# Moving routing work of an expert mixture from VectorE to ScalarE and GpSimd, and delaying work in the last attention unit

## The reference

```python
z = jnp.einsum('nd,sdr->nsr', xf, P)            # xf: layernorm of h; S=8 spaces, R=16
scores = jnp.einsum('nsr,smr->nsm', z, C)       # M=64 experts a space
topv, topi = jax.lax.top_k(scores, K)           # K=4
w = jax.nn.softmax(topv, axis=-1)
...
h = jax.nn.gelu(jnp.einsum('nsr,nskrh->nskh', z, W1g) + b1g)
yl = jnp.einsum('nskh,nskhr->nskr', h, W2g) + b2g
comb = jnp.einsum('nskr,nsk->nsr', yl, w)
out = jax.nn.gelu(comb @ G1 + g1b) @ G2 + g2b
```

## Time and profile before

| | us |
|---|---|
| median of 3 runs | 2743.81 |
| lowest, highest | 2742.77, 2745.2 |
| the profiled execution | 2734.5 |
| its span | 2732.8 |

### The profile page before, as it was taken

One profiled execution on the slowest core, in us unless ns is written; L12 is line 12 of the kernel. 1 busy time (PEld: TensorE's weight loads), 2 busy tenths in 40 slices (PEclk: granted clock), 3 DMA queues, 4 the chain that ended last, 5 costly groups with the idle time before them and its releaser, 6 DMA issues. The chain is left out here.

```text
span 2732.8 us, 42139 instructions
## 1 busy us (share of the span) xinstructions
PE 2409.2 (88%) x16000; PEld 1217.6 (45%) x16000; DVE 1920.0 (70%) x3888; ACT 1211.1 (44%) x1624; POOL 1142.5 (42%) x774
## 2 busy tenths in 40 slices
PE   3475899999999999999999999767988898898888
PEld 1132565555555555655555555433233232232332
DVE  5873675656565565656565656658889989989998
ACT  3332233333333333333333333345666667677766
POOL 5000275757575766667575757451112111211010
PEclk9787999999999999999999999987899999999999
DMA  1002000000001000000000010220000000000000
GB/s 48 12 16 65 1 8 9 1 9 1 9 1 32 1 9 1 9 2 8 9 1 3 1 19 1 42 62 20 20 15 19 8 19 20 14 18 9 18 7 7
DMA packets 43081, 39.42 MB, mean 14 GB/s; under 512 B 26880, under 2 KB 35328, under 8 KB 41984
## 3 DMA queue, kind: packets, MB, share of 16 engines
q1 hardware_dynamic: 40608, 31.18, 5.1%
q0 software_dynamic: 1536, 3.15, 0.4%
q10 hardware_dynamic: 736, 2.41, 0.2%
HBM read 26.23 MB, written 10.49 MB: 13 GB/s over the span
## 5 line engine op out<-in xcount | busy, mean ns | idle before, releaser
L661 POOL TENSOR_TENSOR acc<-acc,pT 128x1024 f32<-128x1024 f32 (+3 forms) x412 | 835.6, 2028 | 245.5 <-ACT pT L1059 208.4
L1059 ACT ACTIVATE pT<-banks 128x1024 f32<-128x1024 f32 x480 | 406.6, 896 | 835.3 <-PE banks L734 765.6
L1759 DVE TENSOR_TENSOR hw<-hid,banks 128x512 f32<-128x512 f32 x1024 | 665.0, 680 | 74.9 <-PE banks L1454 62.9
L879 DVE TENSOR_REDUCE part<-banks 128x2 f32<-128x1024 f32 (+3 forms) x432 | 438.1, 1044 | 311.6 <-PE banks L710 309.9
L1597 ACT ACTIVATE hid<-banks 128x1024 f32<-128x1024 f32 x512 | 498.5, 1022 | 259.3 <-PE banks L1444 218.7
L1454 PE MATMUL banks<-wT,select 64*128 64x512 f16 x1024 | 358.5, 404 | 74.4 <-DVE hw L1759 49.4
L750 PE MATMUL banks<-pT,v 128*64 128x512 f32 (+3 forms) x1920 | 407.2, 545 | 2.2 <-POOL pT L645 2.2
L1444 PE MATMUL banks<-zst,w1c 50*128 50x512 f32 x1024 | 324.8, 558 | 6.0 <-ACT hid L1597 5.9
L1454 PEld LDWEIGHTS banks<-wT,select 64*128 64x128 f16 x1024 | 95.1, 95 | 456.4 <-DVE hw L1759 368.9
L1462 PE MATMUL banks<-hw,w 128*32 128x512 f32 x2048 | 289.3, 638 | 0.8 <-DVE hw L1759 0.8
L750 PEld LDWEIGHTS banks<-pT,v 128*64 128x64 f32 x1920 | 117.2, 137 | 205.4 <-issue 184.2
(11 more groups left out here) (220 smaller groups left out, 3064.9 us busy)
## 6 DMA issues: line engine op xcount, KB each, us to landing
zst<-z_scratch SPq DMA_DIRECT2D x48, 128.0 KB, 4.1
z_scratch<-zp SPq DMA_DIRECT2D x8, 512.0 KB, 2.8
out_h<-o SPq DMA_DIRECT2D x8, 384.0 KB, 2.6
xT_scratch<-xs_hi SPq DMA_DIRECT2D x4, 512.0 KB, 2.7
xt_hi<-xT_scratch SPq DMA_DIRECT2D x2, 1024.0 KB, 5.6
w<-in_L_ffn_W ACTq DMA_DIRECT2D x1, 2048.0 KB, 8.2
xt_hi<-in_L_ffn_W SPq DMA_DIRECT2D x12, 128.0 KB, 4.4
v<-in_L_ffn_W SPq DMA_DIRECT2D x12, 128.0 KB, 4.7
```

Source lines behind the costliest of these rows:

```text
L661: pool.tensor_tensor(acc[:, G % 2, :, off:CH], acc[:, G % 2, :, off:CH], pT[:, slot, :, 0:w], ALU.add).then_inc(summed, 1)
L879: last = dve.tensor_reduce(to[:, :, c:c + 1], both[:, :, 0:whole], AX.X, ALU.max)
L1059: act.activation(pT[:, J % PSLOTS, :, 0:CH - off], both[:, :, 0:CH - off], ACT.Exp, scale=E ** -0.5)\
L1759: dve.tensor_tensor(hw[:, n % 2, q, :], hid[:, n % 2, q, :], ring_bank(("w", g, n, q)), ALU.mult).then_inc(mixed, 1)
```

## The change

Last attention unit: the output items of chunks 0 to 2 stand six macros behind, not four; prepare(t) stands at the end of VectorE's macro, behind invert and normalise, and most of its pieces in later macros. Experts: row sums and sums of squares go from VectorE (and the square from GpSimd) to ScalarE's accumulating activations, with the small arithmetic of the normalisation and z's split on GpSimd; keep_marked and high_weights go from VectorE to GpSimd as compare, product, product, cast, difference; scores take one bank at a time, in steps 5, 7, 9, 11; z's items stand in steps 14, 15, 17; ScalarE empties the output banks, and g2's bias becomes a 65th row of g2 against a row of ones in gh.

```diff
-        X2_AT, Z_AT = (6, 7), 8
-        NORMALISE_AT = {1: 0, 2: 1, 3: 2, 5: 3}
-        ONES_AT, SPLIT_Z_AT = 4, 9
-        POWER_BEHIND = 8
-        PART_AT = {5: None, 6: 0, 9: 1, 12: 2, 15: 3}
+        X2_AT, Z_AT = (9, 10), 11
+        NORMALISE_AT = {0: 0, 1: 1, 2: 2, 6: 3}
+        ONES_AT, SPLIT_Z_AT = 7, 13
+        POWER_BEHIND = 10
+        PART_AT = {8: None, 9: 0, 12: 1, 14: 2, 16: 3}
+
+        OUT_BEHIND = [4] * LAST + [6]
...
-                unit, t = divmod(it * MACROS + LASTKEY[Q] // 2 + 4, MACROS)
+                unit, t = divmod(it * MACROS + LASTKEY[Q] // 2 + OUT_BEHIND[it], MACROS)
...
                     if it == LAST:
                         sum_odd(2 * t + 1)
-                        prepare(t)
                     if behind(it, t, 2):
                         invert(*behind(it, t, 2), 0)
                     if behind(it, t, 3):
                         invert(*behind(it, t, 3), 1)
                         normalise(*behind(it, t, 3))
+                    if it == LAST:
+                        prepare(t)
...
-        Z_AT = {13: (0,), 14: (1,), 15: (2,)}
-        PREP_AT = {5: (3, 4), 7: (5, 6), 23: (7,), 24: (8,), 26: (9,), 27: (10,)}
+        Z_AT = {14: (0,), 15: (1,), 17: (2,)}
+        PREP_AT = {5: (3,), 7: (4,), 9: (5,), 11: (6,), 23: (7,), 24: (8,), 26: (9,), 27: (10,)}
...
-        KEEP_AT = {(20, 1): 0, (20, 3): 1, (21, 1): 2, (22, 1): 3}
-        HIGH_AT = {(22, 0): 0, (24, 0): 1}
         DEN_AT, RECIPROCALS_AT = (16, 0), (20, 0)
-        SUMS_AT, VARIANCE_AT, REFINE_AT, SPLIT_AT = (6, 0), (8, 0), (10, 0), (18, 0)
-        TAKE_OUT_AT = {(3, 1): 0, (4, 1): 1}
+
+        SUM_AT = {4: 0, 5: 1, 6: 2, 7: 3}
+        SQUARE_AT = {8: 0, 9: 1, 10: 2, 11: 3}
...
             def centre(g):
...
+                pool.wait_ge(summed, g)
+                link(pool.tensor_scalar(neg_mean, total, -1.0 / D, None, ALU.mult))
+                pool.sem_inc(mean_ready, 1)
+                link(pool.tensor_tensor(tok(c[:, :]), tok(h_all[:, g * GW:(g + 1) * GW]), wide(neg_mean), ALU.add))
...
             def scale(g):
-                pool.wait_ge(rstd_ready, g)
+                pool.wait_ge(squared, g)
+                link(pool.tensor_scalar(var, var, 1.0 / D, LNEPS, ALU.mult, ALU.add))
+                link(pool.tensor_tensor(rstd, var, power[:, :], ALU.pow))
+                link(pool.tensor_tensor(newton, rstd, rstd, ALU.mult))
+                link(pool.tensor_tensor(newton, newton, var, ALU.mult))
+                link(pool.tensor_scalar(newton, newton, -0.5, 1.5, ALU.mult, ALU.add))
+                link(pool.tensor_tensor(rstd, rstd, newton, ALU.mult))
                 pool.tensor_tensor(tok(x2[:, :]), tok(c[:, :]), wide(rstd), ALU.mult).then_inc(xn_ready, 1)
...
+            def make_weights(g, part):
...
+                pool.wait_ge(rows_marked, 2 * g + part + 1)
+                pool.tensor_scalar(scr[:, half, 0:M], scr[:, half, 0:M], TAKEN, None, ALU.is_equal)\
+                    .then_inc(kept_step, 1)
+                pool.wait_ge(kept_step, done + 1)
+                pool.wait_ge(exp_done, g + 1)
+                pool.tensor_tensor(ew[:, half, :], ew[:, half, :], scr[:, half, 0:M], ALU.mult).then_inc(kept_step, 1)
+                pool.wait_ge(kept_step, done + 2)
+                pool.wait_ge(rden_ready, g + 1)
                 pool.tensor_tensor(ew[:, half, :], ew[:, half, :],
                                    rden[:, 1, half].unsqueeze(2).to_broadcast([P, GT * S // 2, M]), ALU.mult)\
...
+                pool.tensor_copy(wsp[:, half, :, 0, :], by_half).then_inc(kept_step, 1)
+                pool.wait_ge(kept_step, done + 4)
                 pool.tensor_tensor(wsp[:, half, :, 1, :], by_half, wsp[:, half, :, 0, :], ALU.subtract)\
                     .then_inc(w_ready, 1)
...
                 if g < NG - 2:
-                    normalise(g + 2)
+                    centre(g + 2)
+                    scale(g + 2)
                 if g < NG - 1:
-                    weights(g + 1)
+                    below_best(g + 1)
+                if g < NG - 2:
+                    split_z(g + 2)
+                if g < NG - 1:
+                    for part in range(2):
+                        make_weights(g + 1, part)
...
+            def sum_rows(g, t):
+                if t == 0 and g > 1:
+                    act.wait_ge(xn_ready, g - 1)
+                last = act.activation(sq[:, t * D:(t + 1) * D], h_all[:, (g * GT + t) * D:(g * GT + t + 1) * D],
+                                      ACT.Identity, accum_out=total[:, t:t + 1])
...
+            def square_rows(g, t):
+                if t == 0:
+                    act.wait_ge(mean_ready, g)
+                last = act.activation(sq[:, t * D:(t + 1) * D], h_all[:, (g * GT + t) * D:(g * GT + t + 1) * D],
+                                      ACT.Square, bias=neg_mean[:, t:t + 1], accum_out=var[:, t:t + 1])
...
+            def take_out(g, k):
+                if k == 0:
+                    act.wait_ge(out_stored, g * 16 + 16)
+                bank = bank_in(("out", g, 1 + k))
+                act.activation(tok(o[:, :])[:, 2 * k:2 * k + 2, :],
+                               bank.rearrange("p (t n) -> p t n", t=2)[:, :, 0:D], ACT.Copy).then_inc(out_taken, 1)
...
+            for t in range(GT):
+                sum_rows(1, t)
             for item in FIRST_ITEMS[:4]:
                 take(*item)
+            for t in range(GT):
+                square_rows(1, t)
...
                     if n == EXP_AT and g < NG - 1:
                         exponentials(g + 1)
+                    if n in SUM_AT and g < NG - 2:
+                        sum_rows(g + 2, SUM_AT[n])
+                    if n in SQUARE_AT and g < NG - 2:
+                        square_rows(g + 2, SQUARE_AT[n])
```

More of the change, by code:

```diff
@@ L1197, in stage_experts @@
         comb = sb("comb", [P, GTOK])
-        gh = sb("gh", [GH, GTOK])
-        mean, var, rstd, newton = (small[:, GT * i:GT * i + GT] for i in range(4))
+        gh = sb("gh", [GH + 1, GTOK])
+        total, neg_mean, var, rstd, newton = (small[:, GT * i:GT * i + GT] for i in range(5))
         tok = lambda a: a.rearrange("p (n d) -> p n d", d=D)
@@ L1350, in add_input @@
                 pool.tensor_tensor(o[:, :], o[:, :], h_all[:, g * GW:(g + 1) * GW], ALU.add).then_inc(out_ready, 1)
-            def normalise(g):
-                centre(g)
-                root(g)
-                scale(g)
-            def weights(g):
-                below_best(g)
-                for part in range(2):
-                    divide(g, part)
-                    low_weights(g, part)
             centre(1)
@@ L1365, in _ @@
             pool.wait_ge(selected, 7)
-            root(1)
             scale(1)
@@ L1369, in _ @@
             pool.wait_ge(ones_ready, 2)
+            split_z(1)
             for g in range(NG):
@@ L1407, in make_z, with score @@
                 pe.matmul(bank, pm_lo[:, :], xt_lo[:, :], start=False, stop=True).then_inc(side_full, 1)
-            def score(g, u, t2):
-                banks = [bank_free(("prep", g, 3 + 2 * t2 + half)) for half in range(2)]
-                if t2 == 0:
+            def score(g, u, k):
+                t2, half = divmod(k, 2)
+                bank = bank_free(("prep", g, 3 + k))
+                if k == 0:
                     need(pe, z_in, g * 96)
+                rows = slice(HALF * half, HALF * half + ZR)
                 for t in (2 * t2, 2 * t2 + 1):
@@ L1415, in score @@
                         to = ((t % 2) * NQ + q) * M
-                        for half in range(2):
-                            rows = slice(HALF * half, HALF * half + ZR)
-                            last = pe.matmul(banks[half][:, to:to + M], zst[rows, u, q, t * P:(t + 1) * P],
-                                             cm[rows, q, :], start=True, stop=True)
-                last.then_inc(side_full, 2)
+                        last = pe.matmul(bank[:, to:to + M], zst[rows, u, q, t * P:(t + 1) * P], cm[rows, q, :],
+                                         start=True, stop=True)
+                last.then_inc(side_full, 1)
             def turn_w(g, k):
@@ L1644, in _ @@
                         exponentials(g + 1)
+                    if n in SUM_AT and g < NG - 2:
+                        sum_rows(g + 2, SUM_AT[n])
+                    if n in SQUARE_AT and g < NG - 2:
+                        square_rows(g + 2, SQUARE_AT[n])
             take_mixture(NG - 1)
-            mixture_gelu(NG - 1)
+            for k in range(OUT_ITEMS):
+                take("out", NG - 1, k)
         @block.vector
@@ L1733, in mark @@
             def mark(g, i):
+                if g and i == 0:
+                    dve.wait_ge(w_ready, 2 * g)
                 last = dve.match_replace(scr[:, i, :], top[:, i, :], sc[:, i, :], TAKEN)
-                if i % (GT * S // 4) == GT * S // 4 - 1:
-                    link(last)
+                if i % (GT * S // 2) == GT * S // 2 - 1:
+                    last.then_inc(rows_marked, 1)
```

(22 more changed lines are left out.)

93 lines of the change are left out of this document (35 added, 58 removed).

## The result

| | before | after |
|---|---|---|
| median of the runs | 2744.1 us (4 runs, 2742.8 to 2745.2) | 2675.6 us (4 runs, 2674.9 to 2676.8) |
| ratio to before, 95% interval | | 0.9751 [0.9735, 0.9766] |
| profiled execution | 2734.5 us | 2675.9 us (span 2674.1) |

The change takes off 68 us of the median; 2674 was forecast. Two single executions, 6059 us in a later experiment and 6508 us of the kernel before beside another, lie far outside all others and are in no ratio.

The account below looks back on a forecast made before the run. Bounds: VectorE in the experts' groups, TensorE's waits for VectorE's oT in the last attention unit. Experts 48.5, attention 20, start 1.5 make 70 us: 2734.5 to 2664.5, plus 9.3 gives 2674 us; range 2654 to 2703.

Parts of the forecast that it names:

- Last unit: Last attention unit: waits for oT 15.8 and 1.7 us gone, low clock 4.2, less 2 lost; net 20 us (8 to 23).
- The lag: Last attention unit: keep_part operations moved to macros 12, 14, 16, beside GpSimd's sums, delay the end; taken as 2 us.
- Rival 3: Last attention unit: VectorE and GpSimd, sharing SBUF reads, hold up TensorE; gain there 6, not 20, total 2688 us; chance 0.17.
- Weights 4.9 a group: Experts' steps 20 to 22: keep_marked and the cast leaving VectorE save 1.2, 0.94 and 0.6 + 2.16 us a group.
- Scores singly 3.2 a group: Experts' steps 6 to 12: one score bank a step, row sums and refine gone from VectorE, saves 3.2 us a group.
- the exponentials' slip: Experts' step 19: z's copies ahead of ScalarE's exponentials make it wait 2.0 us in six groups; bounds 0 and 2.8.
- Rival 4: Experts: the delay of ScalarE's exponentials is hidden, 12 us more gain, 2662 us; chance 0.15.
- Step 20 at 3.9: Experts: sign that step 20 falls from 5.10 to 3.9 us once two keep_marked operations leave VectorE.
- rival 2: Experts: Square isn't in ScalarE's gelu table, extra table loads cost 39 us in all, 2713 us; chance 0.03.
- Deadlines: GpSimd's weights chain: compare 1.1 us, cast 1.2; second half lasts 8.8, wanted some 14.4 later, hidden with 5 to spare.
- Rival 1: GpSimd's compare costs far more than a copy, missing the weights' deadline; gain gone from 11 us, 2765 at 12.5; chance 0.03.
- The difference to the median: Whole kernel: the median of runs lay 9.3 us above the profiled execution; carried over from 2664.5 to 2674 us.

## Why the prediction was right, step by step

**Last unit, right (20, measured 19.3).** The oT waits gave 17.0 us where 15.8 + 1.7 were counted, and the clock came back with them. The lag that I took as 2 us is there in another form: 2.7 us of waits for h_all, VectorE late by some more operations. Rival 3 (VectorE and GpSimd slow each other, gain 6) falls by the number, though its sums of 3.4 us are still in the trace. I had read the cause as one order in VectorE; that is so, but the runs showed that the two edits need each other, which the sum didn't say.

**Experts, right in sum (48.5, measured 48.3) and wrong in its parts.** That the two agree to 0.2 us is luck. The same code of before took from 764.9 to 778.2 us in its seven groups, so another pair of profiles would have given anything from 41 to 54; and the terms that fell short were made up for by the clock, which the sum didn't have.
- *Weights 4.9 a group* (34 in seven): the run that takes it back loses 35.9. Right in size, but made up otherwise. In group 4 taking the weights back costs 0.6 in step 20 (1.2 in the sum), 0.95 in step 21, 2.3 in step 22, and 1.25 in step 23, which is clock and wasn't in the sum. The sum also took step 22 down to a bare step, 2.56, where its own terms give 5.15 - 2.76 = 2.4; it takes 2.86.
- *Scores singly 3.2 a group.* The size of the drop in steps 6 to 12 was near (16.4 to 13.9, 2.5), the cause named for it was wrong. I took 1.1 us off each of steps 6 and 8 for a row sum and priced the second bank at what was left. Without row sums doubled scores cost 0.4 a group in the kernel before (its seventh group) and nothing in the changed one; most of the cost was there only with both. How the two hold each other up was not isolated further; in step 6 of the kernel before each mix behind the sum waits about 0.6 us for TensorE's spread (L1454), and the sum itself is 1.1.
- *split_z 0.6, the exponentials' slip -2.0.* The step named is right: step 19 takes 6.27 (forecast 6.1), with one wait of 2.2 us for ScalarE's gelu in it (VectorE's waits in the stage, below). What I left out is that step 16 gets z's price back, 4.50 to 3.40, while step 18 keeps 4.76 against 4.7. Steps 14 to 19 together grew by 0.6, where 1.4 was in the sum. Rival 4, the slip hidden, falls by the 6.27.

```profile
DVE hw L1791 <- ACT hid L1633: 14.4, 8, 2.2
```

- *Step 20 at 3.9.* In five of the first six groups it is 4.7 or more, and 3.9 only in group 2, where TensorE keeps part of its clock; group 2's window below has 0.80, group 4's above 0.50 with 5.03. I had taken the 1.2 us of VectorE out of a step that TensorE at half clock holds at 5.0. The term stood on a row at full clock; in the changed kernel's seventh group, at full clock, the step takes 3.71.

```profile
2126.24:2130.16 3.92, 2.67 (x4) 0.80 0.00 0
```

- *What made up for it* is the clock elsewhere, 93 us at the lower level down to 43. Of the kernel before's six groups with z the quietest took 109.8 us and all six 665.1, 6.3 us over six quiet ones; after, 103.3 (the quietest behind the first) and 623.3, 3.5 over. So the quiet groups give 39 of the 48 us, the shorter seventh group 6.6, and what is left, 2.8, goes with the clock. The quietest groups aren't free of it either (mean clock 0.95 and 0.98), so 2.8 is its least. That clock share is counted, not isolated: no run held the clock and changed nothing else.
- *Output copies 0.3:* nothing, by the run that takes them back. *Row sums on ScalarE at no cost:* right. The seventh group, which has none, takes 3.48 and 3.62 in steps 6 and 8 as the others do, though each sum is followed by a read-out of 0.20 us that I hadn't counted. Square and Identity brought no table load; ScalarE's groups after have 9 and 8 loads, as before. This is rival 2, fallen.

```profile
L1633 ACT ACT_TABLE_LOAD x9 | 11.5, 1283 | 0.2
L1619 ACT ACT_TABLE_LOAD x8 | 10.3, 1283 | 0.1
```

**Deadlines, right with the wrong price.** GpSimd's groups after (count, busy, mean ns):

```profile
L1355 POOL TENSOR_SCALAR scr<-scr 128x1024 f32<-128x1024 f32 x14 | 39.0, 2787 | 15.9 <-DVE scr L1766 15.9
L1359 POOL TENSOR_TENSOR ew<-ew,scr 128x1024 f32<-128x1024 f32 x14 | 33.2, 2373 | 1.2
...
L1362 POOL TENSOR_TENSOR ew<-ew,rden 128x1024 f32<-128x1024 f32 x14 | 26.6, 1903 | 16.3 <-DVE rden L1773 15.7
...
L1368 POOL CAST wsp<-ew 128x1024 f16<-128x1024 f32 x14 | 14.5, 1037 | 0.9
```

The compare takes 2.79 us, not 1.1, above the 1.90 of my upper row. The chain of the second half is 10.6 us and not 8.8, and 4.0 us stay of the 5. Rival 1 needed 11 us for the compare; 2.79 is far from it, and the estimate of 10 us from the Trainium skill (GPSIMD Engine Reference, section 3.1) is not borne out: the 1024 elements took 2.79.

**Start and tail.** The start gave 0.3 where 1.5 was counted, in the experiments too. The tail is right: it lost 1.9 in the profiled execution alone, where TensorE does the last output matmuls at the lower clock (L1510, eight in 2.90 us against 1.53 before), and nothing in six of the seven experiments with this code at the end (1.54 us for the same eight matmuls).

**The signs.** L775's waits (6.9), groups of 103 (103.9 on average), the bare step (2.55) and no VectorE operation of 2.2 us in the groups came out. Step 22 (2.86 for 2.6), step 6 (3.48 for 3.0) and step 20 (5.03 for 3.9) didn't.

**The difference to the median, right and in part luck.** Carrying the 9.3 us over was the step with the least reason behind it. The profile after has no such difference (2675.9 against 2675.6), and 7 of the 9.3 may be the quick start of one execution. Without that carry the forecast would have been 2664.5.

## What to carry to other kernels

Two costs that stand in the same step don't have a price each. Here the second bank of a ring costs 1.8 us a group beside a row sum and 0.4 without one, so a sum of terms came near the total and named the wrong cause; ask of every pair what is left when only one of them goes, and look in the trace for a group that already lacks one. A total that agrees is no proof of its terms: an unchanged stage took 13 us more in one profile than in another, nearly all of it in steps at the lower clock. When an order is changed to remove a wait, look for the next reader of the same engine: moving the output alone turned a wait of 10.2 us for oT into one of 7.4 for the next stage's input. And read TensorE's clock beside every step that is to be shortened, since a VectorE that holds it up can be paid for again in the steps behind.

## What the runs showed of the hardware

- A compare with a constant on GpSimd, 128x1024, one input: 2.79 us; a cast of the same size 1.04, a product with a broadcast operand 1.90, with a full one 2.37. So "one input" says little of the price there.
- Small operations of four elements on GpSimd: 0.20 us, but 1.04 for the power. On ScalarE the row sum's read-out takes another 0.20 us beside each activation of 0.37 to 0.45.
- The lower clock in one step is worth 1.3 us there (step 20: 3.71 at 1.00, 3.92 at 0.80, 5.03 at 0.50), and it falls at step 20 in this kernel with the stall ahead of it and, in most groups, without.
- How much of a stage runs at the lower clock changes from execution to execution of the same code: the seven groups of before took 764.9 to 778.2 us, mean clock 0.95 to 0.93, in four profiles.
- The start of the program, in code that no kernel here changes, took from 306.8 to 321.2 us in 14 profiles.
